# Attention and routed feed-forward on one core: three PSUM banks for the key-major scores, two for the scores of the row maximum

## The chip, the core and the metric

The kernel runs on one core of a Trainium2 chip, in one launch. The metric is the device time of that launch in microseconds. TensorE multiplies matrices and writes into PSUM, which has eight banks here of 128 partitions x 512 fp32 values; ScalarE (ACT) and VectorE (DVE) read PSUM; GpSimd (POOL) works in SBUF; SyncE (SP) issues the DMAs. The engines run on their own and meet at semaphores.

## The reference

For x of shape (2, 2048, 1024), all in fp32:

```python
q = (x @ Wq) in 32 heads of 32;  k, v = x @ Wkv      # one k and one v for all heads
scores = q @ k.T * 32 ** -0.5 + slope[h] * (kpos - qpos)
attn = softmax(where(kpos <= qpos, scores, -inf))
x1 = layernorm(x + (attn @ v) @ Wo)
y = x1 @ W.T + b + the LoRA product of the rank (8, 16, 32 or 64) with the largest gate score
out = layernorm(x1 + y)
```

## The kernel before, in words

`attention` comes first and takes some 3,300 us, `feed_forward` follows. This case touches `attention` only.

The queries of each of the 2 batches are cut into 4 segments s of 512 (`QB`). Within a segment there are 8 units u of 4 heads (`HG`, `GH`), so 64 units in all. Unit (s, u) goes over 4(s+1) steps k, one for each tile of 128 keys up to the diagonal. A step has four slots, one for each head h.

Two kinds of scores are computed in every unit:
- Key-major scores ("S" in the plan). TensorE makes a tile of 128 keys x 512 queries in a bank of `ps_s` (line 771; on the diagonal a mask is added at line 774). ScalarE takes the exponential into `prob` (line 509) and so frees the bank. There are two banks, chosen by the head: `h % 2`. The semaphore `s_full` counts filled banks, `e_done` the exponentials.
- Scores of the row maximum ("A"), query-major, for the next unit. TensorE makes a tile of 128 queries x up to 512 keys in a bank of `ps_a` (line 707, mask line 710). VectorE reduces it to one maximum for each row (line 589) and so frees the bank. There are three banks, taken in turn by `bank_of`. The semaphore `a_full` counts filled banks, `a_done` the reductions.

Each unit also holds: "PV", the product of probabilities and values of step k-1 into `ps_o` (line 794), placed behind the slot h = 1 of step k; "SM" and "SP", the row sums of one step or of a pair of steps into `ps_sum`, at h = 3; "ADD", GpSimd's sum of two probability tiles (line 452); "Q", the projection of the queries of the unit after next into `ps_m` (lines 671 to 673), and "QE", its eviction in four pieces, first by ScalarE (line 481) and then by VectorE (line 582); "R", the reciprocals of the last unit's sums (line 607); "CV" and "CT", the shift that is worked out from the maxima on VectorE (line 596) and turned by TensorE (line 715), whose result the next unit's first score waits for through a DMA.

`plan_step` writes down one order of all these for a unit, and every engine goes through that same list and picks out its own. So each engine works in program order, and what it waits for is set by semaphore counts. The maximum chunks are spread over all slots but the last six or seven. There are 16(s+1) chunks for 4 x 4(s+1) slots, so some slots get two; the last unit of a segment has the chunks of the next, longer segment.

The last four chunks of each head (those on the diagonal) are 128, 256, 384 and 512 keys wide, the others 512. The last unit of segment 3 has no maximum chunks.

`ps_a` serves also as the place where x is turned in segment 0 (`turned_in`: its banks 0 and 1, before any maximum chunk of the batch). Besides the five banks above, `ps_o`, `ps_sum` and `ps_m` have one each, which makes eight.

The lines around the change: the bank of a score tile at 504 (ScalarE) and 765 (TensorE), TensorE's wait ahead of a score matmul at 769, its wait ahead of a maximum matmul at 706, and the PV step at 777 to 782.

Of the kernel before, what the change touches and what calls it, by code (L numbers as in the profile page):

```python
# [14 lines left out]
P = 128  # L15
# [3 lines left out]
GH = P // DH  # L19
HG = NH // GH  # L20
QB = 512
# [25 lines left out]
def ktiles(s):  # L47

    return QT * (s + 1)
# [11 lines left out]
def steps_before(s, u):  # L61
    return HG * sum(ktiles(x) for x in range(s)) + u * ktiles(s)
# [17 lines left out]


def bank_of(count):
    return count % 3


def slot_of(count):
# [95 lines left out]
def attention(nc, sb, pb, sem, slopes, xb, wq_v, wkv, att, slope_rows, ident):  # L182
    with ExitStack() as ctx:
# [37 lines left out]
        r_sb = sb(ctx, "r_sb", [P, QB], F32)  # L221
        at_sb = sb(ctx, "at_sb", [P, QB], F32)

        ps_s = [pb(ctx, f"ps_s{i}", [P, QB]) for i in range(2)]
        ps_a = [pb(ctx, f"ps_a{i}", [P, QB]) for i in range(3)]
        ps_o = pb(ctx, "ps_o", [P, QB])
        ps_sum = pb(ctx, "ps_sum", [P, QB])
        ps_m = pb(ctx, "ps_m", [P, QB])
# [50 lines left out]
        e_done = counter("e_done")  # L279
        a_full = counter("a_full")  # L280
        a_done = counter("a_done")
# [183 lines left out]
        def _(act):  # L465
# [25 lines left out]
            def step(b, s, u, const, plan):  # L491
                g, tiles, steps = counts(act, b, s, u)
                for what, arg in plan:
                    if what == "X":
                        split_x(b, s + 1, arg)
                    if what == "WS":
                        split_wq(g + 3)
                    if what == "QE":
                        take_q(g + 2, parity(s, const + 2), tiles, [arg])
                    if what == "S":  # L500
                        k, h = arg
                        c0 = max(0, k - QT * s) * P
                        slot = slot_of(steps_before(s, const) + k)
                        bank = h % 2
                        act.wait_ge(s_full, tiles + (GH * k + h + 1))
                        if h == 0:
                            early = s == 0 and steps_before(s, const) + k < PROBS
                            act.wait_ge(sm_done, steps + (-steps_before(s, const) if early else k + 1 - PROBS))
                        nc.scalar.activation(prob[slot][:, h, c0:], ps_s[bank][:, c0:], ACT.Exp,  # L509
                                             bias=alibi_of(u, h, k - QT * s)).then_inc(e_done, 1)  # L510
                    if what == "OE":
                        act.wait_ge(sm_done, steps + ktiles(s))
                        act.wait_ge(at_done, START + g)
                        nc.scalar.activation(o_sb[:], ps_o[:], ACT.Copy).then_inc(o_copied, 1)
                        nc.scalar.activation(s_sb[:], ps_sum[:], ACT.Copy).then_inc(o_copied, 1)  # L515
# [132 lines left out]
        def _(pe):  # L648
# [51 lines left out]
            def scores_for_max(g, tiles, first, s, i, chunk, buf, bank):  # L700

                h, t, c, cols = chunk
                ps = ps_a[bank]
                if i == 0:
                    pe.wait_ge(stack_in, START + 32 * (g + 1))
                pe.wait_ge(a_done, tiles + (0 if first and i < 3 else i - 2))
                last = nc.tensor.matmul(ps[:, 0:cols], qst[buf][0:KR, h, t * P:(t + 1) * P],  # L707
                                        kmax[0:KR, c * QB:c * QB + cols], start=True, stop=c < s)
                if c == s:
                    last = nc.tensor.matmul(ps[:, cols - P:cols], identb[:], maskb[:], start=False, stop=True)  # L710
                last.then_inc(a_full, 1)
# [22 lines left out]
            def step(b, s, u, const, plan):  # L734
                g, tiles, steps = counts(pe, b, s, u)
                buf = parity(s, const)
                i = 0
                for what, arg in plan:
# [23 lines left out]
                    if what == "S":  # L762
                        k, h = arg
                        c0 = max(0, k - QT * s) * P
                        bank = h % 2
                        if arg == (0, 0):
                            pe.wait_ge(c_in, START + 16 * (g + 1))
                        early = s == 0 and const == 0 and GH * k + h < 2
                        pe.wait_ge(e_done, tiles + (0 if early else GH * k + h - 1))
                        diagonal = k >= QT * s  # L770
                        last = nc.tensor.matmul(ps_s[bank][:, c0:], kexp[0:KR, k * P:(k + 1) * P],  # L771
                                                qst[buf][0:KR, h, c0:], start=True, stop=not diagonal)
                        if diagonal:
                            last = nc.tensor.matmul(ps_s[bank][:, c0:c0 + P], identb[:], maskt[:], start=False,  # L774
                                                    stop=True)
                        last.then_inc(s_full, 1)
                    if what == "PV":
                        if arg == ktiles(s) - 1:
                            pe.wait_ge(e_done, tiles + GH * (arg + 1))
                        if arg == 0:  # L780
                            pe.wait_ge(o_copied, START + 2 * g)
                        over_keys(s, const, ps_o, val[:, arg], arg).then_inc(pv_done, 1)
# [458 lines left out]
```

## Time and profile before

| | |
|---|---|
| median of 3 runs | 4210.84 us (4203.0, 4215.06, 4210.84) |
| profiled execution, first to last instruction | 4202.6 us |
| TensorE (PE) busy | 3850.6 us, 92% |
| VectorE (DVE) busy | 2472.1 us, 59% |
| ScalarE (ACT) busy | 1929.4 us, 46% |
| GpSimd (POOL) busy | 1359.6 us, 32% |
| mean granted TensorE clock | 0.949 of full speed |

All times below are microseconds from the start of the span. A row of the timeline gives the start, the duration, the engine, the line, the operation and, with xN, how many such instructions are merged into it; in brackets stands the idle time of the engine ahead of it and what ended it. PEld is TensorE's loading of weights, which can run beside a matmul. The granted clock is 1.00 at 2.4 GHz and 0.50 at 1.2 GHz. Matmuls are pipelined, so that two of them overlap in their rows: the distance between two starts tells what one costs.

### The profile page before, as it was taken

Reading aid. Unit: us, or ns where it says so; the run is one execution under the profiler, and the core shown is the slowest. Engines: PE = TensorE matmul, PEld = TensorE weight load, DVE = VectorE, ACT = ScalarE, POOL = GpSimd, SP = SyncE. Lnnn points to the kernel's source line nnn. Section 1 sums busy time; section 2 is a strip of 40 time slices with the busy share of each in tenths; the row PEclk is TensorE's granted clock in tenths of the full one; section 3 lists DMA queues with packets and bytes.
Section 4 is the critical chain, followed back from the end, with each engine's and each line's share of the span. In section 5 each row is a group of like instructions: output and inputs, shape, how many; then the busy total and the mean of one; then the engine's idle time right before and its main releaser. Section 6 shows DMA issues by size and latency. Waiting matters only on the chain. (4 is left out here: it accounts for less than half of the span.)

```text
span 4202.6 us, 73921 instructions
## 1 busy us (share of the span) xinstructions
PE 3850.6 (92%) x22065; PEld 2340.6 (56%) x22065; DVE 2472.1 (59%) x4462; ACT 1929.4 (46%) x3253; POOL 1359.6 (32%) x420
## 2 busy tenths in 40 slices
PE   5989989999999998789999999999999599999998
PEld 3555544444444443555554444544443388888887
DVE  4566666666766672556666656766675244444444
ACT  2445645565666565344555656566565401000000
POOL 1114434444444454112433444445454200000010
PEclk8899989999999998899998999999998799999999
DMA  2111110000000001111001000000000311111111
GB/s 72 47 51 27 28 41 22 20 21 16 19 19 14 19 6 34 54 44 49 26 26 43 19 22 22 14 19 14 19 14 6 131 56 60 60 60 60 60 60 51
DMA packets 159069, 152.11 MB, mean 36 GB/s; under 512 B 8388, under 2 KB 141508, under 8 KB 156584
## 3 DMA queue, kind: packets, MB, share of 16 engines
q1 hardware_dynamic: 158696, 147.70, 11.9%
q8 instruction: 166, 2.72, 0.3%
q14 instruction: 207, 1.70, 0.1%
HBM read 96.75 MB, written 33.62 MB: 31 GB/s over the span
## 5 line engine op out<-in xcount | busy, mean ns | idle before, releaser
L509 ACT ACTIVATE prob<-ps_s,alibi 128x512 f32<-128x512 f32 (+3 forms) x2560 | 1524.5, 623 | 1193.3 <-PE ps_s L774 603.4
L589 DVE TENSOR_REDUCE mxp<-ps_a 128x1 f32<-128x512 f32 (+3 forms) x2560 | 1457.6, 605 | 910.2 <-PE ps_a L707 462.5
L452 POOL TENSOR_TENSOR prob<-prob 128x2048 f32<-128x2048 f32 (+1 forms) x240 | 1043.8, 4349 | 1298.2 <-ACT prob L509 1298.2
L771 PE MATMUL ps_s<-qst,kexp 97*128 97x512 f32 (+3 forms) x2560 | 1107.2, 444 | 84.8 <-ACT prob L509 52.8
L771 PEld LDWEIGHTS ps_s<-qst,kexp 97*128 97x128 f32 x2560 | 504.1, 198 | 905.9 <-ACT prob L509 710.4
L707 PE MATMUL ps_a<-kmax,qst 97*128 97x512 f32 (+3 forms) x2560 | 950.3, 397 | 29.2 <-DMA qst<-qst 13.4
L794 PE MATMUL ps_o<-prob,val 128*32 128x512 f32 (+3 forms) x5120 | 624.8, 562 | 0.0
L707 PEld LDWEIGHTS ps_a<-kmax,qst 97*128 97x128 f32 x2560 | 503.3, 197 | 107.6 <-DVE mxp L589 52.7
L794 PE MATMUL ps_sum<-prob,ones 128*32 128x512 f32 (+3 forms) x3200 | 384.8, 569 | 0.1
L980 POOL TENSOR_TENSOR hb_sb<-h_sb,bias_b 128x1024 f32<-128x1024 f32 x32 | 76.9, 2402 | 790.9 <-DVE z_sb L1124 731.1
L607 DVE RECIPROCAL r_sb<-s_sb 128x128 f32<-128x128 f32 x256 | 233.8, 931 | 122.0 <-ACT s_sb L515 119.8
L1010 ACT ACTIVATE root<-var 128x1 f32<-128x1 f32 x64 | 13.0, 203 | 606.8 <-DVE var L1069 606.8
L433 POOL TENSOR_TENSOR wql<-wq_raw,wqh 128x1024 fp32r<-128x1024 f32 x65 | 154.2, 2372 | 351.8 <-ACT wqh L474 351.5
L1181 PE MATMUL ps_z<-wth,hth 128*128 128x364 f32 x768 | 255.3, 332 | 5.3 <-DVE htl L1136 5.3
L1183 PE MATMUL ps_z<-wtl,hth 128*128 128x364 f32 x768 | 253.3, 330 | 0.0
L1185 PE MATMUL ps_z<-wth,htl 128*128 128x364 f32 x768 | 253.2, 330 | 0.0
L774 PE MATMUL ps_s<-maskt,identb 128*128 128x128 bf16 x1024 | 246.1, 243 | 0.0
L710 PE MATMUL ps_a<-maskb,identb 128*128 128x128 bf16 x1024 | 240.6, 236 | 0.0
L671 PE MATMUL ps_m<-xh,wqh 128*128 128x512 f32 x512 | 222.0, 434 | 7.5 <-POOL wql L433 4.2
L582 DVE SCALAR_TENSOR_TENSOR qst<-ps_m,qst 32x512 fp32r<-32x512 f32 x256 | 176.0, 688 | 86.4 <-ACT qst L481 80.2
L672 PE MATMUL ps_m<-xl,wqh 128*128 128x512 f32 x512 | 211.7, 414 | 0.0
L673 PE MATMUL ps_m<-xh,wql 128*128 128x512 f32 x512 | 210.6, 411 | 0.0
(148 smaller groups left out, 3672.5 us busy)
## 6 DMA issues: line engine op xcount, KB each, us to landing
wq_raw<-in_L_attn_Wq SPq DMA_DIRECT2D x65, 512.0 KB, 3.8
xs<-in_L_attn_hidden_states SPq DMA_DIRECT2D x9, 2048.0 KB, 8.1
qst<-qst SPq DMA_DIRECT2D x64, 256.0 KB
att_scratch<-at_sb SPq DMA_DIRECT2D x64, 256.0 KB, 2.3
at_raw<-att_scratch SPq DMA_DIRECT2D x32, 512.0 KB, 5.4
x_sb<-in_L_attn_hidden_states SPq DMA_DIRECT2D x32, 512.0 KB, 4.3
out<-z_sb SPq DMA_DIRECT2D x32, 512.0 KB, 3.1
z_sb<-in_L_attn_Wo SPq DMA_DIRECT2D x4, 512.0 KB, 5.3
```

The lines of the kernel that those rows point to most:

```text
L452: nc.gpsimd.tensor_tensor(even[:, :, c1:], even[:, :, c1:], odd[:, :, c1:], ALU.add).then_inc(pair_done, 1)
L509: nc.scalar.activation(prob[slot][:, h, c0:], ps_s[bank][:, c0:], ACT.Exp, bias=alibi_of(u, h, k - QT * s)).then_inc(e_done, 1)
L589: nc.vector.tensor_reduce(mxp[:, h * QT + t, c:c + 1], ps_a[bank][:, 0:cols], AX.X, ALU.max).then_inc(a_done, 1)
L607: nc.vector.reciprocal(r_sb[:, cols], s_sb[:, cols]).then_inc(r_done, 1)
L707: last = nc.tensor.matmul(ps[:, 0:cols], qst[buf][0:KR, h, t * P:(t + 1) * P], kmax[0:KR, c * QB:c * QB + cols], start=True, stop=c < s)
L710: last = nc.tensor.matmul(ps[:, cols - P:cols], identb[:], maskb[:], start=False, stop=True)
L771: last = nc.tensor.matmul(ps_s[bank][:, c0:], kexp[0:KR, k * P:(k + 1) * P], qst[buf][0:KR, h, c0:], start=True, stop=not diagonal)
L774: last = nc.tensor.matmul(ps_s[bank][:, c0:c0 + P], identb[:], maskt[:], start=False, stop=True)
L794: last = nc.tensor.matmul(ps[h * DH:(h + 1) * DH, c0:], weights, prob[slot][:, h, c0:], start=k == 0, stop=k == ktiles(s) - 1)
L1181: nc.tensor.matmul(ps, hth[:, c], wth[:, c, piece(p)], start=c == 0, stop=False, skip_group_check=True)
L1183: nc.tensor.matmul(ps, hth[:, c], wtl[:, c, piece(p)], start=False, stop=False, skip_group_check=True)
L1185: last = nc.tensor.matmul(ps, htl[:, c], wth[:, c, piece(p)], start=False, stop=False, skip_group_check=True)
```

## The change

The eight banks are shared out anew. `ps_s` gets three banks, taken in turn by a running count of all score tiles (`score_bank`), and `ps_a` gets two (`bank_of`). The waits follow: a score matmul waits until the exponential three tiles before it is done, instead of two; a maximum matmul waits until the reduction two tiles before it is done, instead of three. The PV step waits for the four exponentials of its own step at every step; before, it did so at the last step of a unit only, as the wait of the score matmul (k, 1) ahead of it covered the others. No other instruction is added, removed or moved.

```diff
 def bank_of(count):
-    return count % 3
+    return count % 2
+
+def score_bank(s, const, k, h):
+    return (GH * (steps_before(s, const) + k) + h) % 3
...
-        ps_s = [pb(ctx, f"ps_s{i}", [P, QB]) for i in range(2)]
-        ps_a = [pb(ctx, f"ps_a{i}", [P, QB]) for i in range(3)]
+        ps_s = [pb(ctx, f"ps_s{i}", [P, QB]) for i in range(3)]
+        ps_a = [pb(ctx, f"ps_a{i}", [P, QB]) for i in range(2)]
...
-                        bank = h % 2
+                        bank = score_bank(s, const, k, h)
...
-                pe.wait_ge(a_done, tiles + (0 if first and i < 3 else i - 2))
+                pe.wait_ge(a_done, tiles + (0 if first and i < 2 else i - 1))
...
-                        bank = h % 2
+                        bank = score_bank(s, const, k, h)
...
-                        early = s == 0 and const == 0 and GH * k + h < 2
-                        pe.wait_ge(e_done, tiles + (0 if early else GH * k + h - 1))
+                        early = s == 0 and const == 0 and GH * k + h < 3
+                        pe.wait_ge(e_done, tiles + (0 if early else GH * k + h - 2))
...
-                        if arg == ktiles(s) - 1:
-                            pe.wait_ge(e_done, tiles + GH * (arg + 1))
+                        pe.wait_ge(e_done, tiles + GH * (arg + 1))
```

## Rows read from the trace of the kernel before

**Rows 1.** The page, part 1: busy us, share of the span, instructions of each engine.
```profile
PE 3850.6 (92%) x22065; PEld 2340.6 (56%) x22065; DVE 2472.1 (59%) x4462; ACT 1929.4 (46%) x3253; POOL 1359.6 (32%) x420
```

**Rows 2.** Stretches: us, PE, PEld, DVE, ACT, POOL busy, PEclk, DMA share, GB/s; segment 2.
```profile
646.30:1109.30 463.00, 435.54 (x2521) 223.91 (x2517) 308.78 (x501) 270.10 (x448) 202.80 (x56) 0.96 0.08 20
```

**Rows 3.** Waits, whole span: who waited for whom, us in total, times, longest.
```profile
PEld ps_s L771 <- ACT prob L509: 710.4, 1033, 4.0
...
PE ps_s L771 <- ACT prob L509: 52.8, 124, 3.6
PEld ps_a L707 <- DVE mxp L589: 52.7, 135, 1.5
```

**Rows 4.** Timeline, a long run of segment 3, all engines.
```profile
1280.47 0.50 PE L771 MATMUL ps_s<-qst,kexp 97*128 97x512 f32 x1
...
1280.81 0.39 PE L707 MATMUL ps_a<-kmax,qst 97*128 97x512 f32 x1
...
1281.20 1.27 ACT L509 ACTIVATE prob<-ps_s,alibi 128x512 f32<-128x512 f32 x2 [0.79 <-PE ps_s L771]
1281.23 1.29 DVE L589 TENSOR_REDUCE mxp<-ps_a 128x1 f32<-128x512 f32 x2 [0.83 <-PE ps_a L707]
1281.27 0.40 PE L707 MATMUL ps_a<-kmax,qst 97*128 97x512 f32 x1
...
1281.94 0.50 PE L771 MATMUL ps_s<-qst,kexp 97*128 97x512 f32 x1 [0.28 <-ACT prob L509]
...
1283.30 1.06 PE L794 MATMUL ps_o<-prob,val 128*32 128x512 f32 x8
```

**Rows 5.** Timeline, the start of a unit of segment 2.
```profile
759.38 0.73 PE L707 MATMUL ps_a<-kmax,qst 97*128 97x512 f32 x2
...
759.92 2.55 DVE L589 TENSOR_REDUCE mxp<-ps_a 128x1 f32<-128x512 f32 x4 [6.18 <-PE ps_a L707]
...
760.17 0.40 PE L707 MATMUL ps_a<-kmax,qst 97*128 97x512 f32 x1
```

**Rows 6.** Timeline, Q evictions in the same unit.
```profile
777.79 0.40 PE L707 MATMUL ps_a<-kmax,qst 97*128 97x512 f32 x1
...
778.71 1.09 PE L707 MATMUL ps_a<-kmax,qst 97*128 97x512 f32 x2
...
779.28 0.69 DVE L582 SCALAR_TENSOR_TENSOR qst<-ps_m,qst 32x512 fp32r<-32x512 f32 x1
779.30 0.19 PEld L707 LDWEIGHTS ps_a<-kmax,qst 97*128 97x128 f32 x1 [0.41 <-DVE mxp L589]
...
779.73 1.07 PE L794 MATMUL ps_o<-prob,val 128*32 128x512 f32 x8
780.00 1.29 DVE L589 TENSOR_REDUCE mxp<-ps_a 128x1 f32<-128x512 f32 x2
```

**Rows 7.** Timeline, a burst in the last unit of segment 0.
```profile
276.53 0.94 PE L707 MATMUL ps_a<-kmax,qst 97*128 97x512 f32 x3
...
277.04 1.89 DVE L589 TENSOR_REDUCE mxp<-ps_a 128x1 f32<-128x512 f32 x3
```

**Rows 8.** Timeline, the last unit of segment 3, PE and then ACT.
```profile
1629.13 0.78 PE L771 MATMUL ps_s<-qst,kexp 97*128 97x512 f32 x2
1630.41 1.08 PE L771 MATMUL ps_s<-qst,kexp 97*128 97x512 f32 x2 [0.51 <-ACT prob L509]
1631.42 1.06 PE L794 MATMUL ps_o<-prob,val 128*32 128x512 f32 x8
...
1629.67 2.62 ACT L509 ACTIVATE prob<-ps_s,alibi 128x512 f32<-128x512 f32 x4 [0.32 <-PE ps_s L771]
```

**Rows 9.** Timeline, the shift at the end of a unit of segment 2.
```profile
807.84 0.28 PE L715 MATMUL ps_m<-ident,shift 128*16 128x128 f32 x1 [1.70 <-DVE shift L596]
```

**Rows 10.** Stretches of two units each in segment 3, columns as in rows 2.
```profile
1109.30:1246.80 137.50, 130.88 (x774) 64.17 (x770) 94.34 (x150) 87.23 (x142) 69.06 (x18) 1.00 0.06 17
1246.80:1394.90 148.10, 139.42 (x774) 67.93 (x770) 94.35 (x150) 87.48 (x142) 69.01 (x18) 0.93 0.07 19
```

## Prediction

> **What bounds the kernel now.** I read the page first: TensorE is busy for 92% of the span, VectorE for 59%, ScalarE for 46% [rows 1]. The table by stretch shows the same inside a stage: in query segment 2 of the first batch TensorE is busy 435.54 of 463.00 us, VectorE 308.78, ScalarE 270.10 [rows 2]. So TensorE is the bound, and what a bank change is worth must be read as gaps between starts of matmuls. The list of waits overstates them: the weight loads of `ps_s` wait 710.4 us for the exponential, but the matmul array itself idles only 52.8 us for it [rows 3], because most of that wait runs beside the probability x value products. The timeline tells the rest. Three facts are read there, in a run of segment 3 [rows 4]:
> - Unhindered, one 512-column matmul starts 0.23 us after another (1280.81 to 1281.27 with a score matmul between). Behind a probability product or behind a wait the weights are not loaded ahead, and the next one starts 0.34 us later (1280.47 to 1280.81).
> - A score tile holds its bank long: the matmul starts at 1280.47, its exponential runs from 1281.20 to 1281.84 (half of 1.27), and the third score matmul starts at 1281.94. Its predecessor started at 1281.27, so it could have started at 1281.50: 0.44 us lost, and 0.11 more for the unhidden load behind it. This is what a third score bank is for.
> - A maximum tile does the same on VectorE: matmul at 1280.81, reduction from 1281.23 to 1281.87. With three banks that never stops TensorE here.
>
> **What the change does.** It adds and removes no matmul, no DMA and no work on any engine; only waits of TensorE move. (a) A score matmul waits for the exponential three before it. (b) A maximum matmul waits for the reduction two before it; queued behind that wait on TensorE are score matmuls, Q projections and the probability products, so ScalarE and, through it, GpSimd's pair sums wait too. (c) Each PV step now has its own wait for the last exponential of its step. Before, the score matmul (k, 1) ahead of it waited for the same exponential, so (c) costs nothing new; it only moves that wait behind the matmuls between. The queues of SyncE and GpSimd issue the same things in the same order and pass nothing. With few exponentials outstanding (a) gives nothing, so I price both by the place where they bite. `qst` evictions pass through ScalarE and VectorE in program order, which matters in term 2.
>
> **1. Start of a unit.** Two maximum matmuls start at 759.38, a third at 760.17. The reductions run back to back from 759.92, 0.64 us each (2.55 for four) [rows 5]. With two banks the third waits for the first reduction: 759.92 + 0.64 + 0.05 = 760.61, which is 0.44 later, and 0.11 for the unhidden load: +0.55 us. Nothing covers it, as Q projections on TensorE follow. It holds for the units of segments 1 to 3 with full-width maximum chunks, 23 a batch, and the last unit of segment 0: 48 x 0.55 = **+26 us**.
>
> **2. The Q evictions.** VectorE must do four `qst` subtractions in order between reductions. At 779.28 one runs 0.69 us, and the reductions behind it start at 780.00 (1.29 for two). The first of these serves the maximum matmul of 777.79; two more matmuls started at 778.71 and 779.30, and TensorE is at the product (PV) at 779.73 [rows 6]. With two banks the matmul of 779.30 needs the tile of 777.79 reduced: 780.00 + 0.64 = 780.64. That is 1.34 us later. The third score bank does not bring VectorE forward, since VectorE works without a break here. The other waits of the cluster partly fall in the place of score waits that go; by stepping through the cluster of one unit of each segment I get a net 0.16 more, so 1.5 us a unit. Units of segments 1 to 3 with Q work: 22 a batch. 44 x 1.5 = **+66 us**. In segment 0 the chunks are short; I take 0.65 for 16 units: **+10 us**. Bounds: 0 (VectorE catches up and the wait only replaces the stall at the shift, below) and 2.5 a unit (all of VectorE's lag lands on TensorE), 0 to 110 us.
>
> **3. Long runs with five maximum matmuls.** Between two products (PV) of every second step come four score matmuls, and every eighth slot holds an extra maximum matmul. In [rows 4], the third score matmul now starts at 1281.50. The next maximum matmul needs the reduction of 1280.81's tile: 1281.87 + 0.05 = 1281.92. The one behind needs the second reduction, 1282.52: 1282.57. Then score at 1282.91, the fifth maximum matmul after the third reduction (1283.16) at 1283.21, and the product 0.43 later (as 779.30 to 779.73 in [rows 6]) at 1283.64. It was 1283.30 [rows 4]. So where the score wait alone would give a gain of 0.55, I get +0.35 us (rounded up from 0.34). Three such runs in each of 14 units of segment 3, two in 16 of segment 2, one in 16 of segment 1: 90 x 0.35 = **+31 us**.
>
> **4. Runs near the diagonal.** There the chunks are 128 to 384 wide, reductions are short, and only the score wait is left. A gain of 0.55 for a wide run as in [rows 4], and by my estimate 0.25 for a narrow one: 0.8 in 14 units, 0.65 in 16, 0.25 in 16: **-25 us**.
>
> **5. Last unit of segments 0, 1, 2.** It holds the next segment's chunks in bursts: three matmuls at 276.53 with reductions from 277.04, 1.89 for three [rows 7]. The third must wait for 277.67 + 0.05 instead of starting at 277.08: 0.64 and 0.11 for the load, four or five times. Beyond terms 1 and 2, 3 us a unit: **+18 us**.
>
> **6. Last unit of segment 3.** No maxima at all. Scores at 1629.13 (and 0.34 later), then stalled to 1630.41 and 0.58 later, product at 1631.42 [rows 8]. With three banks the third starts at 1629.70, the fourth after the first exponential (1629.67 + 0.66 + 0.05 = 1630.38), the product after the second (1631.03): -0.35, some eight runs in two units: **-6 us**. Next late is ScalarE, whose four exponentials take 2.62.
>
> **The end of a unit** absorbs something: TensorE sits 1.70 us before the transpose of the shift, until VectorE is through with it [rows 9]. Score stalls removed between the last maximum matmul and there are worth nothing, and I counted none. Lateness of the last maximum matmul is not absorbed, since the shift follows it.
>
> **7. The clock.** Two units of segment 3 took 137.50 us at granted clock 1.00, the next two 148.10 at 0.93, with the same matmuls (774) [rows 10]: 5.3 us a unit. TensorE's clock falls to 1.2 GHz behind stalls such as the one of [rows 9], and the cluster of term 2 becomes such a stall. Unseen in the trace; bounds 0 and 36 x 5.3 = 190 us. I take a tenth, nearest to the undisturbed units: **+20 us**.
>
> The Trainium skill has a rule here, in "TensorE: Matmul & The Clock Gate", section "A second HAM failure mode: psum-queue depth-cycling": a kernel that cycles through PSUM banks idles often for short times, and its clock then swings between the two levels. This trace shows the swing behind longer stalls only; by the rule term 7 would go toward its upper end. The same page ("Step-by-step: what each phase is for") has weights pulled ahead of running matmuls; by that alone the 0.11 us behind each wait would vanish. The rows show it, and I count it.
>
> **The sum.** 26 + 66 + 10 + 31 - 25 + 18 - 6 + 20 = 140 us on the profiled span of 4202.6 us: 4342.6. The median of the runs shown, 4210.84, is 8.2 above that span: 4351 us, 3.3% slower.
>
> **Rivals.**
> - *Scores win* (faster). Every long run gains 0.55 us and the reductions are never last. Seven, five and three long runs a unit in segments 3, 2, 1, 16 units each: 240 x 0.55 = 132, with term 6 138: 4073 us. For it speaks that ScalarE ends the wait in the run shown, and that VectorE as a whole is idle a third of the stretch. It decides if reduction 1 of a run ends before its third maximum matmul is due: 1281.87 against 1281.73, a miss of 0.14 us in a run, but of 1.34 in a cluster. 6%.
> - *They cancel*: terms 1 to 3 shrink to the size of 4 and 6 since VectorE's lag hides behind the end of the unit: 4211. 4%.
> - *The clusters are absorbed*, term 2 and 7 fall away: 140 - 96 = 44: 4255. 8%.
> - *The third score bank does nothing*, since the PV step waits for the same exponential as the score matmul did: terms 4 and 6 are lost, 140 + 31: 4382. 12%.
> - *The clock answers* in half of the units, term 7 is 95: 4426; in all, 4521. 12%.
> - The forecast itself: 58%.
>
> The range reaches from 4265, just above the case of absorbed clusters, to 4440. The chances, with 0.3% about what a measurement of this kernel can tell from no change: faster 0.06, same 0.04, slower 0.90.
>
> **What would show it.** Right: waits of `ps_a` on VectorE's reductions, now 52.7 us on weight loads [rows 3], grow severalfold; the third maximum matmul of a unit starts 0.4 us later; the waits of `ps_s` on ScalarE shrink; the last unit of segment 3, without maxima, gets shorter; segments 1 and 2 lose the larger share, and the second half of the kernel, from 3296 us on, keeps its length. Term 2 is wrong if the matmul ahead of the product in an eviction cluster does not wait. Term 7 shows in the granted clock, 0.96 in segment 2 now [rows 2]. The prediction is wrong if the long runs get shorter with the extra maximum matmul in them, or if TensorE's busy share of segment 2 rises.

## The result, and the profile after

| | before | after |
|---|---|---|
| median of 4 runs each | 4209.77 us (4203.0 to 4215.06) | 4381.53 us (4367.8 to 4391.07) |
| profiled execution, first to last instruction | 4202.6 us | 4371.0 us |
| TensorE busy | 3850.6 us, 92% | 3927.8 us, 90% |
| mean granted TensorE clock | 0.949 | 0.945 |

The changed kernel takes 1.0404 [1.0377, 1.0432] of the time of before: slower by 172 us, 168 in the profiled executions. 4351 was forecast, in a range of 4265 to 4440.

After, the page, part 1 (against [rows 1]) and the table by stretch (against [rows 2]); the two stretches are segments 2 and 3 of the first batch, in the order us, PE, PEld, DVE, ACT, POOL busy, granted clock, DMA share, GB/s:

```profile
PE 3927.8 (90%) x22065; PEld 2341.8 (54%) x22065; DVE 2509.9 (57%) x4462; ACT 1915.4 (44%) x3253; POOL 1358.3 (31%) x420
```

```profile
671.57:1166.01 494.44, 445.29 (x2521) 223.02 (x2517) 317.05 (x501) 269.02 (x448) 202.61 (x56) 0.96 0.07 19
1166.01:1752.00 585.99, 540.86 (x2955) 247.01 (x2951) 340.37 (x529) 337.42 (x560) 272.34 (x71) 0.94 0.06 17
```

The counts of instructions are those of before; TensorE has the same 2521 matmuls in segment 2 and 31 us more to do them in. ScalarE is less busy than before although it has the same exponentials. What has grown is the distance between starts. The list of waits (who <- for whom: us in total, times, longest) names the engine behind it; against [rows 3]:

```profile
PEld ps_s L776 <- ACT prob L514: 478.1, 600, 1.8
PEld ps_a L712 <- DVE mxp L594: 378.6, 636, 1.7
PE ps_a L712 <- DVE mxp L594: 143.1, 276, 1.6
```

and the line of before that answers to the third:

```profile
PE ps_a L707 <- DVE mxp L589: 11.3, 20, 1.3
```

The weight loads of score tiles wait 232 us less for the exponential, those of maximum tiles 326 us more for the reduction. The weight load's wait runs beside other matmuls, so the third line says more: the array itself stood 143.1 us for a reduction; before this was 11.3 us, in 20 places. TensorE's busy share of segment 2 falls from 94% to 90%.

Where the 168 us are, from the first score matmul of each unit to that of the next, after minus before, in us a unit:

| segment | units 0 to 5 | unit 6 | unit 7 | both batches |
|---|---|---|---|---|
| 0 | -0.5 | +4.1 | +7.2 | +16 |
| 1 | +2.0 | +2.3 | -0.4 | +28 |
| 2 | +3.8 | +3.9 | +6.8 | +67 |
| 3 | +5.0 | +3.6 | -7.0 | +53 |

(Means over the units of both batches, in the profiled executions. The last unit of segment 3 is taken from its first to its last score matmul.) The rest, 4 us, lies at the start, between the batches, and 0.5 us in `feed_forward` (from the last score matmul to the end 909.2 us before, 909.7 after).

These numbers hold what the clock did in that one execution too. From here on "at half clock" is the time that the trace's record of the granted clock has at 0.50, from the start to the last score matmul: 369 us before, 416 after. Two prices for it are read below, 0.33 and 0.5 us lost for each us at half clock.

**The places themselves.** The first row of each group of the timeline answers to a row of before. Start of a unit of segment 2 (against [rows 5]):

```profile
787.97 0.63 PE L712 MATMUL ps_a<-kmax,qst 97*128 97x512 f32 x2
788.40 1.97 DVE L594 TENSOR_REDUCE mxp<-ps_a 128x1 f32<-128x512 f32 x3 [4.42 <-PE ps_a L712]
...
789.14 0.50 PE L712 MATMUL ps_a<-kmax,qst 97*128 97x512 f32 x1 [0.31 <-DVE mxp L594]
789.48 0.42 PE L676 MATMUL ps_m<-xh,wqh 128*128 128x512 f32 x1
```

The third maximum matmul starts 1.17 behind the first, before 0.79 (759.38 to 760.17), and the Q projection behind it 0.34 later instead of 0.23: 0.49 us together. A long run of segment 3 with five maximum matmuls (against [rows 4], which is the same run):

```profile
1354.92 0.50 PE L776 MATMUL ps_s<-qst,kexp 97*128 97x512 f32 x1
...
1355.68 3.26 DVE L594 TENSOR_REDUCE mxp<-ps_a 128x1 f32<-128x512 f32 x5 [0.83 <-PE ps_a L712]
...
1355.95 0.39 PE L776 MATMUL ps_s<-qst,kexp 97*128 97x512 f32 x1
1356.43 0.19 PEld L712 LDWEIGHTS ps_a<-kmax,qst 97*128 97x128 f32 x1 [0.52 <-DVE mxp L594]
...
1357.71 0.19 PEld L712 LDWEIGHTS ps_a<-kmax,qst 97*128 97x128 f32 x1 [0.39 <-DVE mxp L594]
...
1358.15 0.64 PE L798 MATMUL ps_o<-prob,val 128*32 128x512 f32 x4
```

The third score matmul now starts 1.03 after the first (1355.95), before 1.47: the third score bank works. But VectorE's reductions now run five in a row without a break, and each later maximum matmul stands until one of them ends. The product comes at 3.23 after the first score matmul; before at 2.83. An eviction cluster of segment 3, PE, ACT and DVE (the one of [rows 6] lies in segment 2):

```profile
1337.95 0.59 ACT L486 ACTIVATE qst<-ps_m 32x512 fp32r<-32x512 f32 x1
...
1338.57 0.69 DVE L587 SCALAR_TENSOR_TENSOR qst<-ps_m,qst 32x512 fp32r<-32x512 f32 x1 [0.35 <-ACT qst L486]
...
1339.29 1.98 DVE L594 TENSOR_REDUCE mxp<-ps_a 128x1 f32<-128x512 f32 x3
1340.04 0.50 PE L712 MATMUL ps_a<-kmax,qst 97*128 97x512 f32 x1 [1.03 <-DVE mxp L594]
1340.47 1.06 PE L798 MATMUL ps_o<-prob,val 128*32 128x512 f32 x8
```

TensorE stands 1.03 us for a reduction, the reduction stands behind VectorE's part of the eviction, and that stood 0.35 us for ScalarE's copy. In before the same eviction waited too, for 0.20 us, and the product started 0.43 behind the last maximum matmul, whose row has no stall in brackets: three banks bridged the gap.

```profile
1266.51 0.50 PE L707 MATMUL ps_a<-kmax,qst 97*128 97x512 f32 x1
1266.65 0.69 DVE L582 SCALAR_TENSOR_TENSOR qst<-ps_m,qst 32x512 fp32r<-32x512 f32 x1 [0.20 <-ACT qst L481]
1266.94 1.07 PE L794 MATMUL ps_o<-prob,val 128*32 128x512 f32 x8
```

A burst of the last unit of segment 0 (against [rows 7], three matmuls in one row) and the shift of a unit of segment 3 (against [rows 9]):

```profile
279.58 0.71 PE L712 MATMUL ps_a<-kmax,qst 97*128 97x512 f32 x2
...
280.85 0.50 PE L712 MATMUL ps_a<-kmax,qst 97*128 97x512 f32 x1 [0.55 <-DVE mxp L594]
...
1385.91 0.38 PE L720 MATMUL ps_m<-ident,shift 128*16 128x128 f32 x1 [1.93 <-DVE shift L601]
```

The last unit of segment 3, which has no maximum matmuls (against [rows 8]):

```profile
1724.10 0.96 PE L776 MATMUL ps_s<-qst,kexp 97*128 97x512 f32 x3
...
1725.38 0.50 PE L776 MATMUL ps_s<-qst,kexp 97*128 97x512 f32 x1 [0.32 <-ACT prob L514]
1725.96 1.06 PE L798 MATMUL ps_o<-prob,val 128*32 128x512 f32 x8
```

Three scores start at once instead of two, and the product comes 1.86 us behind the first of them, before 2.29 (1629.13 to 1631.42).

### The profile page after: what moved, and what is told of

It is laid out like the page before. It is cut to its first block and busy times, and to the rows that moved or that the text cites. A ratio compares the mean times of both kernels' runs of the same rounds, so it can differ in the third digit from the quotient of the medians.

```text
span 4371.0 us, 74495 instructions
## 1 busy us (share of the span) xinstructions
PE 3927.8 (90%) x22065; PEld 2341.8 (54%) x22065; DVE 2509.9 (57%) x4462; ACT 1915.4 (44%) x3253; POOL 1358.3 (31%) x420
## 3 DMA queue, kind: packets, MB, share of 16 engines
q8 instruction: 172, 2.82, 0.3%
## 5 line engine op out<-in xcount | busy, mean ns | idle before, releaser
L594 DVE TENSOR_REDUCE mxp<-ps_a 128x1 f32<-128x512 f32 (+3 forms) x2560 | 1486.2, 606 | 1004.0 <-PE ps_a L712 559.0
L712 PE MATMUL ps_a<-kmax,qst 97*128 97x512 f32 (+3 forms) x2560 | 1028.8, 419 | 168.8 <-DVE mxp L594 143.1
L776 PE MATMUL ps_s<-qst,kexp 97*128 97x512 f32 (+3 forms) x2560 | 1074.6, 433 | 31.4 <-issue 14.9
L798 PE MATMUL ps_sum<-prob,ones 128*32 128x512 f32 (+3 forms) x3200 | 398.0, 586 | 0.5 <-issue 0.3
L1177 PE MATMUL ps_y<-woh,ath 128*128 128x512 f32 x512 | 207.1, 404 | 3.9 <-DVE atl L1061 3.9
```

The source lines that it names most:

```text
L594: nc.vector.tensor_reduce(mxp[:, h * QT + t, c:c + 1], ps_a[bank][:, 0:cols], AX.X, ALU.max).then_inc(a_done, 1)
L798: last = nc.tensor.matmul(ps[h * DH:(h + 1) * DH, c0:], weights, prob[slot][:, h, c0:], start=k == 0, stop=k == ktiles(s) - 1)
L1177: nc.tensor.matmul(ps, ath[par][:, c], woh[:, c, cols], start=first, stop=False)
```

## The experiments

The theory: two maximum banks make VectorE's reductions a bound inside every run of matmuls, and the third score bank gives back little. "Distance" below is a changed kernel against its own partner without the bank change. Times are medians.

**1. Which of the two banks costs, which gives.** `a2s2` has two maximum banks and two score banks; one bank is idle.

```diff
-    return count % 3
+    return count % 2
...
-        ps_a = [pb(ctx, f"ps_a{i}", [P, QB]) for i in range(3)]
+        ps_a = [pb(ctx, f"ps_a{i}", [P, QB]) for i in range(2)]
...
-                pe.wait_ge(a_done, tiles + (0 if first and i < 3 else i - 2))
+                pe.wait_ge(a_done, tiles + (0 if first and i < 2 else i - 1))
```

> Two banks for the maxima as in the changed kernel, but also only two for the key-major scores (one of the eight banks lies idle), and the score and PV waits as before. Theory (VectorE's reductions behind two banks make the cost, the third score bank gives some of it back near the diagonal and in the last unit of segment 3, which got 7.0 us shorter in the changed kernel): 4381 + 14 for the two last units + 25 for the diagonal runs = 4420 us, 4400 to 4450. Rival 1 (the third score bank does nothing outside the last unit of segment 3, since the PV step waits for the same exponential): 4395 us. Rival 2 (not the maxima but the PV step's own wait and the new order of score waits make the cost): this kernel has neither and stays within 40 us of 4210.

Measured: 4420.23 us, 1.0507 [1.0491, 1.0524], the 4420 of the theory. The bank taken from the maxima costs 209 us by itself; the third score bank gives 39 back. Both hold some clock: `a2s2` has 464 us at half clock, 96 more than before and 48 more than the changed kernel, which is 32 to 48 of the 209 and 16 to 24 of the 39. It keeps the old PV wait, so the loss does not come from the new wait (c) of the prediction. Units 0 to 5 of segment 3 are +5.6 us each, where the full change has +5.0. In its long run, the one of [rows 4] again, both waits are there, 0.28 us of the array for the exponential and then 0.59 us of the weight load for the reduction:

```profile
1368.00 0.50 PE L771 MATMUL ps_s<-qst,kexp 97*128 97x512 f32 x1 [0.28 <-ACT prob L509]
...
1369.51 0.19 PEld L707 LDWEIGHTS ps_a<-kmax,qst 97*128 97x128 f32 x1 [0.59 <-DVE mxp L589]
...
1369.94 0.64 PE L794 MATMUL ps_o<-prob,val 128*32 128x512 f32 x4
```

The run started at 1366.53, so the product comes after 3.41 us: 2.83 before, 3.23 with the third score bank. The same run thus prices both banks, +0.58 and -0.18.

**2. The third score bank with no bank taken.** The row sums are put into the bank of `ps_o`, in `alias_s2a3` with before's division (a control) and in `alias_s3a3` with three banks for each kind. The sums and the products share a bank and so are mixed up.

```diff
-        ps_sum = pb(ctx, "ps_sum", [P, QB])
+        ps_sum = ps_o
...
-                                            start=k == 0, stop=k == ktiles(s) - 1)
+                                            start=k == 0 and not sums, stop=k == ktiles(s) - 1 and sums)
```

> Control for the next run. Banks and waits as before, but the row sums accumulate in the bank of the products, which leaves one bank idle; the output is then not the attention (products and sums are added up), while every instruction is kept. All theories: 4210 us, within 0.3%.

> The row sums accumulate in the bank of the products, as in the control, and the bank so freed makes three for the scores AND three for the maxima. The third score bank alone, with no bank taken from the maxima. Theory (each long run gains 0.55 us where reductions are not last; 240 such runs, and 7 us in each last unit of segment 3): 110 to 150 us under the control, about 4080 us. Rival (the third score bank does nothing because the PV step waits for the same exponential): only the 14 us of the last units, about 4195 us.

Measured: the control 4216.54 us, 0.9996 [0.9977, 1.0015], so the aliasing itself is free. `alias_s3a3` 4162.74 us, 0.9901 [0.9884, 0.9919]: 54 us under the control. Neither the 110 to 150 us of the one theory nor the 14 us of the other. The waits (the control's two lines, then the two with six banks) and the long run tell why:

```profile
PEld ps_s L771 <- ACT prob L509: 714.9, 1034, 3.9
PEld ps_a L707 <- DVE mxp L589: 53.0, 135, 1.5
```

```profile
PEld ps_s L776 <- ACT prob L514: 538.9, 693, 2.7
PEld ps_a L712 <- DVE mxp L594: 134.4, 341, 1.5
```

```profile
1267.47 0.50 PE L776 MATMUL ps_s<-qst,kexp 97*128 97x512 f32 x1
...
1268.23 2.48 DVE L594 TENSOR_REDUCE mxp<-ps_a 128x1 f32<-128x512 f32 x4 [0.83 <-PE ps_a L712]
...
1270.00 0.64 PE L798 MATMUL ps_o<-prob,val 128*32 128x512 f32 x4
```

2.53 us for the run that took 2.83: a gain of 0.30, not 0.55. As soon as the scores no longer stand, the maxima catch up with VectorE even with three banks (2.48 us for four reductions, one every 0.62), and the wait changes sides: the weight loads wait 81 us more for the reductions. The two profiled executions are 67 us apart. The -9.6 us of each last unit of segment 3, where there are no maxima, makes 19 of them, and more than half of that is the clock (term 6 below); units 0 to 5 of segment 3 give 2.0 each, those of segments 1 and 2 0.7. In all the control has 399 us at half clock and this kernel 355, which is 15 to 22 of the 67.

**3. Is it VectorE's time on the eviction?** In `before_noqd` and `after_noqd` VectorE's part of a Q eviction covers 8 of 512 columns, the rest stays zero.

```diff
-                    nc.vector.scalar_tensor_tensor(qst[buf][2 * DH:3 * DH, h], ps_m[h * DH:(h + 1) * DH], SCALE,
+                    nc.vector.scalar_tensor_tensor(qst[buf][2 * DH:3 * DH, h, 0:8], ps_m[h * DH:(h + 1) * DH, 0:8], SCALE,
```

> The kernel before, but VectorE's part of the Q eviction takes 8 of 512 columns (the low part of the queries is left out for the rest, so the scores are less exact); ScalarE's copies and all waits stay. Partner of the next run. Both theories: somewhat faster than before, 4150 to 4205 us, since VectorE loses 252 x 0.6 us of work and some of it stood ahead of maxima.

> The changed kernel with the same shortened part of the Q eviction. What counts is the distance to its partner, 172 us for the full kernels. Theory (VectorE's lag in the eviction clusters, term 2, reaches TensorE through the second maximum bank): the distance falls by 50 to 80 us, to about 105 us. Rival (the cost lies in bursts and long runs alone, whatever else VectorE does): 150 to 175 us.

Measured: 4141.28 us, 0.9818 [0.9773, 0.9864], and 4289.59 us, 1.0187 [1.015, 1.0224]. The distance is 148 us, not the 105 expected; by it the rival, that it stays at 150 to 175, is nearer. But the two differ by 102 us at half clock (287 and 389), where before and after differ by 48, so this distance holds 16 to 27 us more of clock than theirs. What the cluster itself costs is in the table of 4. The work on the eviction is nearly gone, and TensorE still stands in the cluster:

```profile
1302.67 0.59 ACT L486 ACTIVATE qst<-ps_m 32x512 fp32r<-32x512 f32 x1
...
1303.30 0.17 DVE L589 SCALAR_TENSOR_TENSOR qst<-ps_m,qst 32x8 fp32r<-32x8 f32 x1 [0.59 <-ACT qst L486]
1303.49 1.98 DVE L596 TENSOR_REDUCE mxp<-ps_a 128x1 f32<-128x512 f32 x3
1304.24 0.50 PE L714 MATMUL ps_a<-kmax,qst 97*128 97x512 f32 x1 [0.75 <-DVE mxp L596]
```

0.52 us were taken off VectorE's instruction; VectorE waits 0.24 us longer in front of it (0.59 for 0.35) and TensorE's stall falls by 0.28 (1.03 to 0.75). The copy, at 1302.67, comes right behind two exponentials in ScalarE's queue, which ran from 1301.38 for 1.27 us.

**4. Or the wait in its queue?** In `before_lateqd` and `after_lateqd` VectorE takes its part of the eviction four slots later, so that it never stands for the copy.

```diff
+                late = []
...
-                        take_q(g + 2, parity(s, const + 2), [arg])
+                        late.append([arg, 4])
+                    if what == "S":
+                        late = [[h, left - 1] for h, left in late]
+                    while late and (late[0][1] == 0 or what == "CV"):
+                        take_q(g + 2, parity(s, const + 2), [late.pop(0)[0]])
```

> The kernel before, but VectorE does its part of each Q eviction four slots later in its own order, so that it no longer stands at ScalarE's copy while reductions are due behind it; nothing else moves. Partner of the next run. Theory (this standing is what fills the maximum banks in the eviction clusters): already with three maximum banks some 1 us a unit is won in 44 units, about 4165 us. Rival (VectorE's total work in the cluster is what counts): 4210 us, within 10.

> The changed kernel with the same later part of the Q evictions. What counts is the distance to its partner, 172 us for the full kernels, 148 with the shortened subtraction. Theory (head-of-line wait of VectorE for ScalarE's copy makes the cluster's cost of 1.8 us a unit, 44 units): distance about 95 us, 75 to 120. Rival (VectorE's work, or two banks as such): distance over 140.

Measured: 4255.2 us, 1.0098 [1.0081, 1.0116], and 4363.47 us, 1.036 [1.0341, 1.0379]. The distance falls from 172 to 108 us, within the 75 to 120 of the theory. This alone would say that it is the wait and not the work, but the clock must come off first. In the profiled executions the distances are 168.5 us for the full kernels, 155.3 in 3 and 109.2 here, with 48, 102 and 14 us more at half clock than the partner; at 0.5 us for each, 145, 104 and 102 us are left. The products tell the same. How late is the product behind the eviction cluster, and behind the long runs that lie in it, from the unit's first score matmul, changed kernel against its own partner (difference of the medians over units 0 to 5 of both batches)?

| product behind h = 1 of | full kernels | 3, less work | 4, later |
|---|---|---|---|
| segment 1, step 5 | 2.40 | 1.77 | 1.51 |
| segment 2, step 7 | 3.74 | 2.82 | 2.69 |
| segment 3, step 5 | 2.63 | 1.49 | 1.95 |

So 0.7 to 1.1 us a unit goes when VectorE no longer stands for the copy, and 0.6 to 1.1 when most of its work on the eviction goes. Both count, about alike; these pairs don't divide the cost between them, and that the distance fell by 64 us here and by 24 in 3 is mostly the clock.

For before itself both expectations missed, a gain of 45 us and no change: it loses 44. The order itself does next to nothing there: the products of units 0 to 5 of segments 1 to 3 move by -0.4 to +0.3 us. The kernel has 113 us more at half clock (481), 70 of them in segment 0, which at 0.33 to 0.5 us each is all that it loses. In units 1 to 5 of segment 0 TensorE is idle for 1.57 us ahead of the transpose of the shift instead of 1.29. The first 230 us of segment 0 and what follows, in `before_lateqd` and in before:

```profile
80.00:310.00 230.00, 209.53 (x1238) 131.49 (x1238) 122.56 (x232) 99.92 (x183) 25.44 (x14) 0.82 0.18 53
```

```profile
80.00:309.00 229.00, 206.86 (x1328) 129.41 (x1329) 132.50 (x249) 106.62 (x198) 27.88 (x15) 0.91 0.20 58
```

In about the same time it does 90 matmuls fewer. The smaller distance does not come from this partner's bad segment 0: the distance of segment 0 alone is +14 us for +16.

**5. Is it the reductions' time?** In `before_halfred` and `after_halfred` the reductions off the diagonal read half of their columns; the maxima of the other half are left out.

```diff
-                nc.vector.tensor_reduce(mxp[:, h * QT + t, c:c + 1], ps_a[bank][:, 0:cols], AX.X,
+                nc.vector.tensor_reduce(mxp[:, h * QT + t, c:c + 1], ps_a[bank][:, (0 if whole else cols // 2):cols], AX.X,
```

> The kernel before, but the reduction of every chunk off the diagonal reads 256 of its 512 columns (the maximum is then that of half the keys there); matmuls and waits stay. Partner of the next run. VectorE's reductions shrink from 0.69 to about 0.42 us. Theory: 4180 to 4210 us, as the score banks keep the long runs where they are.

> The changed kernel with the same halved reductions. Theory (what a maximum bank waits for is the time of VectorE's reductions in a row): the distance to the partner falls from 172 us to under 60, and the third score bank may even win. Rival (two banks cost by the latency from matmul to reduction and back, 0.43 + 0.05 us, whatever a reduction takes): the distance stays above 120 us.

Measured: 4179.28 us, 0.9918 [0.9894, 0.9941], and 4278.21 us, 1.0145 [1.0095, 1.0194]. The distance is 99 us, between the under 60 of the theory and the over 120 of the rival. Where nearly all reductions became short, in units 0 to 5 of segment 3, it falls from 5.0 to 0.9 us a unit. In segment 2 it keeps 2.1 of 3.8, in segment 1 1.8 of 2.0, and in units 6 and 7 of segment 0 5.1 and 5.7 us. These means hold the clock too. The lateness of the last product but one, which it moves less, falls from 3.19 to 0.99 us in segment 3, from 2.93 to 1.36 in segment 2 and from 2.17 to 1.78 in segment 1. So the reductions' time is shown as the cause of most of segment 3's loss and of about half of segment 2's. That the chunks of the diagonal, left whole, and the eviction clusters make the rest fits this but was not tested by itself.

**6. Can two banks be served better?** In `after_spread` the double slots are placed four slots later in segments 1 to 3, so that no unit starts with a double chunk and the five fall in other runs.

```diff
-        at.setdefault(i * a_slots // len(chunks), []).append(("A", x))
+        at.setdefault((i * a_slots + (28 if s and sa == s else 0)) // len(chunks), []).append(("A", x))
```

> The changed kernel, with the extra maximum chunks of units of segments 1 to 3 four slots later, so that a unit no longer starts with two chunks in its first slot, and those of segment 3 fall into short runs (behind a row sum) instead of long ones. Theory (term 1: a burst of three maximum matmuls at the start costs 0.5 us, without it nothing, 44 units; the long runs win 0.7 us each, but the short ones lose 0.8, since a third maximum matmul in a row waits there too): 20 to 35 us under the changed kernel, about 4355 us. Rival (term 3 as the place matters: only long runs suffer): 60 us or more under it, 4320 us or less.

Measured: 4295.23 us, 1.0184 [1.0163, 1.0204], 86 us under the changed kernel; 20 to 35 were expected, 60 or more by the rival. One short and one long run of segment 3, from score matmul to product each (it answers to [rows 4], four slots on):

```profile
1331.78 0.50 PE L776 MATMUL ps_s<-qst,kexp 97*128 97x512 f32 x1
...
1333.28 0.51 PE L712 MATMUL ps_a<-kmax,qst 97*128 97x512 f32 x1 [0.32 <-DVE mxp L594]
1333.72 1.06 PE L798 MATMUL ps_o<-prob,val 128*32 128x512 f32 x8
1334.72 0.50 PE L776 MATMUL ps_s<-qst,kexp 97*128 97x512 f32 x1
...
1337.26 0.64 PE L798 MATMUL ps_o<-prob,val 128*32 128x512 f32 x4
```

The long run takes 2.54 instead of 3.23 us, the short one 1.94 instead of 1.14: the local sums (-0.7, +0.8) hold and cancel. The start of the unit is won back, 0.55 us, as summed. What was not summed is the place where a double chunk meets an eviction. From the product of step 2 to the one behind the cluster the lateness against before grows by 0.96 and 1.73 us in segments 1 and 2, where it was 1.88 and 3.18; in segment 3 it grows by 2.05, as it did (2.02). So the double chunks in the clusters cost 0.9 and 1.5 us a unit in segments 1 and 2. The rest of the gain can't be placed: the two profiled executions are only 57 us apart, not 86, and this kernel has 27 us less at half clock. In segment 0, where the edit changes nothing, it takes 15 us longer than the changed kernel with 37 us more at half clock, so a segment's figure from one trace is no surer than that.

**7. Which division is better than both?** `five_banks` is before, but in the last unit of segment 3, where `ps_a` is idle, the scores use all five banks. `late_five` has this and the later eviction of 4.

```diff
+        ps_all = ps_s + ps_a
+
+        def score_ps(s, const, k, h):
+            if s == NSEG - 1 and const == HG - 1:
+                return ps_all[(GH * k + h) % 5]
+            return ps_s[h % 2]
```

> The kernel before, but in the last unit of segment 3, which has no maxima, the scores take all five banks in turn, and the PV step has its own wait there. Theory (the score wait is all that stalls that unit): at least the 7.0 us a unit of the changed kernel, and some 2 us more by the fourth and fifth bank, two units: 4210 - 18 = 4192 us, ratio 0.9957. Rival (beyond three banks the PV wait for its own step's exponentials is last, so the fourth and fifth give nothing): 4210 - 14 = 4196 us.

> The kernel before with both findings: all five banks for the scores in the last unit of segment 3, and VectorE's part of the Q evictions four slots later. Theory: the two add up, 0.9976 from the banks and about 0.989 from the order: ratio 0.987, about 4155 us, better than both kernels of the case. Rival (the later eviction is worth nothing): 0.9976.

Measured: `five_banks` 4199.54 us, 0.9976 [0.9959, 0.9993], the only version here that computes the same and is faster than before, by 10 us. The last unit of segment 3 gives 8.7 us, twice, of which 3.9 are the bank's and the rest is clock (term 6 below). 4192 us were expected and 4196 by the rival. The rival, that banks beyond the third give nothing, is shown: the one of the two units that has nothing at half clock takes 46.95 us with five banks, and with three it takes 46.94. `late_five` 4229.1 us, 1.0038 [1.0022, 1.0054], where 0.987 was expected: in segment 0 it has 142 us at half clock over both batches, `before_lateqd` 136, before 66.

## Why the prediction held, point by point

**Sign and mechanism** were right: VectorE's reductions take the place of ScalarE's exponentials as what comes last, and the sum of 140 us stands against 168. The sum is closer than its parts. By segment, terms 1 to 6 come to +17, +40, +40 and +23 us for segments 0 to 3; measured are +16, +28, +67 and +53, the clock included. Some of the errors cancel, and that is luck. Lateness below is that of the table in 4.

**Term 1, start of a unit.** +0.55 forecast; the first product is late by 0.54 in segment 1, 0.55 in segment 2, 0.60 in segment 3. Right.

**Term 2, Q evictions, was mis-sized and half misread.** From the product of step 2 to the one behind the cluster the lateness grows by 1.88, 3.18 and 2.02 us in segments 1, 2 and 3. Less the long runs of term 3 in it (one, two and none, 0.40 each; in segments 1 and 2 no rise is left for them behind it) this is 1.5, 2.4 and 2.0 us, where 1.5 was forecast for all: over 16, 16 and 12 units 24 + 38 + 24 = 86 us, for 66. The step that failed is "VectorE works without a break here": I took one eviction of four, the third of a unit of segment 2, for all. At the other three of the same unit VectorE stands for ScalarE's copy in before already, for 0.46, 0.14 and 0.32 us, and after for 0.46, 0.54 and 0.61. And a double chunk lies in the clusters of segments 1 and 2 (experiment 6: 0.9 and 1.5 us a unit), which I hadn't told apart.

**Term 3, long runs.** +0.35 forecast; +0.40 in the run shown (3.23 against 2.83), and the products of segment 3 grow late by the same step at each of the three runs (2.63, 3.02, 3.44, 3.85). 36 us, for 31: right.

**Term 4, runs near the diagonal.** -0.8, -0.65 and -0.25 a unit forecast in segments 3, 2 and 1; the lateness falls by 0.67 from step 11 to step 14 in segment 3, by 0.81 from step 7 to step 10 in segment 2 and by 0.23 from step 5 to step 6 in segment 1: -26 us for -25. Right.

**Term 5, last unit of segments 0 to 2.** 3 us a unit beyond terms 1 and 2, so some 4 to 5 with them; +7.2, -0.4 and +6.8 measured: 4.5 in the mean, but not where I put it. In segment 0 the third matmul of the burst shown starts 0.95 behind the second instead of 0.23: 0.72, as worked out (0.75). But it happens more often than four or five times: TensorE stands for 0.55 us ahead of a maximum matmul four times and for 0.62 to 1.04 three times, where before it stood for more than 0.5 once (1.33).

**Term 6, last unit of segment 3.** -3 us a unit forecast, -7.0 measured, and almost half of it isn't the bank's. Before has 17.1 us at half clock in this unit in either batch, the changed kernel 10.2 and 6.8. Its first half, before and after:

```profile
1598.40:1628.00 29.60, 26.38 (x98) 7.94 (x94) 3.39 (x4) 18.70 (x30) 12.59 (x3) 0.71 0.03 9
```

```profile
1691.90:1717.40 25.50, 23.67 (x103) 7.67 (x102) 3.39 (x4) 18.56 (x31) 12.79 (x3) 0.80 0.00 1
```

Some runs have this unit with no half clock at all, with the same instructions, and these price the bank by itself. From the first to the last score matmul, `a2s2` (two score banks) and `alias_s3a3` (three):

```profile
3456.15:3507.02 50.87, 44.78 (x251) 15.40 (x247) 3.39 (x4) 38.30 (x64) 31.41 (x8) 1.00 0.00 1
```

```profile
1575.05:1621.99 46.94, 42.94 (x251) 14.74 (x247) 3.39 (x4) 37.17 (x64) 31.03 (x8) 1.00 0.02 7
```

The third score bank gives 3.9 us, for 3. (`before_noqd` has 50.88 in its first batch; `after_lateqd`, `after_halfred` and `after_spread` have 46.93 to 46.95 in one batch each.) The other 3.1 of the 7.0 us are the clock: with 17.1 us at half clock the unit takes 56.6 us in before, 5.7 more than without, which is 0.33 us for each. In [rows 8] and its line of after the bank gives 0.43 in a run of four scores, for 0.35.

**Segment 0.** +0.65 a unit forecast; -0.5 in the mean of units 0 to 5, -0.1 in the median: the short chunks cost nothing. The +10 us stand in unit 6 instead (+4.1 a unit, 8 in all), which I hadn't told apart; it has 8.6 us more at half clock in either batch, which could be all of it.

**Term 7, the clock.** +20 us forecast. A price first: the 10.6 us between the stretches of [rows 10] go with 148.1 x (1 - 0.93) x 2 = 21 us at half clock, 0.5 us for each; in the last unit of segment 3, where TensorE stands more, it was 0.33. From before to after the time at half clock grows by 48 us (-10, -7, +31 and +34 in segments 0 to 3): some +16 to +25 us, so the term was right in size. Two pairs of units of segment 3, against [rows 10]:

```profile
1166.01:1318.47 152.46, 143.24 (x775) 66.95 (x771) 96.38 (x150) 86.24 (x142) 68.92 (x18) 0.93 0.06 17
1318.47:1471.20 152.73, 140.25 (x750) 67.28 (x750) 96.13 (x150) 86.67 (x142) 68.95 (x18) 0.94 0.05 14
```

No pair of units is at 1.00 any more. The growth lies in two places. One is the eviction clusters, as the term had it. In units 0 to 5 of segments 1 to 3 TensorE's longest stall is 0.83 to 1.17 us in each of the 36 clusters, where it was at most 0.20 before, and in 8 of the 36 the clock falls: 44 us at half clock between the last slot of step 3 and the end of step 5, where before has none. The other is the end of the units of segment 3. Units 0 to 6 have 45 us at half clock behind the transpose of the shift before and 84 after, over both batches. That is what a unit of segment 3 still loses behind step 14 (1.5 us in the mean of units 0 to 5). Elsewhere the time at half clock fell, in segment 0 and in the last unit of segment 3 above all. TensorE's idle time ahead of the transpose is 1.93 us in units 0 to 5 of segments 1 to 3, where it was 1.70. It goes with the third score bank: `a2s2` has 1.70, `alias_s3a3` 1.93, so it is the room that a score stall just ahead of it used to take. The swing that the Trainium skill describes in "TensorE: Matmul & The Clock Gate", section "A second HAM failure mode: psum-queue depth-cycling", would have asked for the upper end of the term; the trace shows its lower quarter. The same page of the Trainium skill, section "Step-by-step: what each phase is for", has weights pulled ahead of running matmuls. The trace agrees where nothing waits, 0.23 us from start to start, and not behind a wait: 0.34 us to the next start, as at 789.14 to 789.48.

**The rivals.** *Scores win* falls, and not only by the two maximum banks: with a bank to spare for them (`alias_s3a3`) the gain is 54 us and not 138. *They cancel* and *the clusters are absorbed* fall with the median of 4381.53. *The third score bank does nothing* comes within 1 us of the median (4382), by chance: `a2s2` shows it worth 39 us, clock included, and what made the time is above all term 2. *The clock answers* needed 95 us of clock and got some 16 to 25.

## What to carry over

Before a bank is moved between two consumers, write down for each how long one tile holds its bank and how often one comes within the densest run, not within the stage: VectorE, busy 59% of the span, was the bound inside every run of five tiles. A third bank for one stream is worth little if the other stream's tiles, in the same in-order queue of TensorE, become due at once (0.30 of 0.55 us a run). Look also at what stands at the head of the consumer's own queue: an instruction that waits for a third engine holds up bank releases as its own work does, and a spare bank is what bridges that. And before two kernels' times are set against each other to find a cause, compare their time at half clock, or a unit that has none in either: three verdicts here changed by it (experiments 3 and 4, term 6).

## What the runs showed of the hardware

In sum the clock moved more between kernels than its causes seemed to. A kernel with 0.52 us less in each eviction (`before_noqd`) had 287 us at half clock instead of 369, some 27 to 41 of its 69 us of gain; one with a later eviction had 481. And the same unit, the last of segment 3, ran its first half at 0.71 in before and at 0.80 after, with no stall there that tells the two apart, and at 1.00 in others; with 17.1 us at half clock it takes 56.6 us, with none 50.9.

In the eviction clusters the clock falls with two maximum banks only. None of the eight kernels with three of them has the clock fall in a cluster of the 36 units above; each of the six with two has: in 8 clusters (the changed kernel), 19 (`a2s2`), 12 (`after_halfred`), 5 (`after_lateqd`), 4 (`after_noqd`) and 2 (`after_spread`). Why in 8 of the changed kernel's 36, when the others have as long a stall, is open.

The fall behind the transpose is not explained by the idle time ahead of it. In units 0 to 5 of segment 3 it came in 8 of 12 units before, with 1.70 us, and in 12 of 12 after, with 1.93. But in segment 1 the same 1.70 and 1.93 us went with 8 of 12 in both kernels, and in segment 3 of `after_halfred`, with 1.93 us too, it came in 8 of 12. What decides it is open.
